# Second graph layer of a GNN and mixture-of-experts kernel: the order of its work on three engines, skewed by one group of tiles

## The reference

```
h = relu(einsum('ts,bsh->bth', adj, x @ Wg0 + bg0))
h = relu(einsum('ts,bsh->bth', adj, h @ Wg1 + bg1))
for p in range(1, MAX_SKIP + 1):
    nw = Tv // p
    wins = h[:, :nw * p, :].reshape(Bv * nw, p, Hd)
    last = _lstm_last(Wih[p - 1], Whh[p - 1], bih[p - 1], bhh[p - 1], wins)
    idx = jnp.arange(nw) * p + (p - 1)
    h = h.at[:, idx, :].set(last.reshape(Bv, nw, Hd))
```

## Time and profile before

| | us |
|---|---|
| median of 3 runs | 1905.67 |
| lowest, highest | 1901.71, 1909.65 |
| the profiled execution | 1909.74 |
| its span, first to last instruction | 1907.9 |
| of it the stage `gnn1` (first gather to end of the last new_state) | 870.31 to 1129.79, 259.5 |
| TensorE, VectorE, ScalarE, POOL busy over the span | 70%, 49%, 34%, 24% |

### The profile page before, as it was taken

One profiled execution on the slowest core, in us unless ns is written; L12 is line 12 of the kernel. 1 busy time (PEld: TensorE's weight loads), 2 busy tenths in 40 slices (PEclk: granted clock), 3 DMA queues, 4 the chain that ended last, 5 costly groups with the idle time before them and its releaser, 6 DMA issues. The chain is left out here.

```text
span 1907.9 us, 25858 instructions
## 1 busy us (share of the span) xinstructions
PE 1332.4 (70%) x5892; PEld 904.9 (47%) x5893; DVE 932.2 (49%) x3988; ACT 655.3 (34%) x1514; POOL 452.5 (24%) x670
## 2 busy tenths in 40 slices
PE   2333410197498999994777779988886998699910
PEld 1223300166466999993434433444333433689910
DVE  6888899776694222223566523333336222701122
ACT  3444400032103455542333335444435433055500
POOL 0000011000004556555655300000000000055556
PEclk9999955596598999996787789999995998599965
DMA  9100000001101222231111000000000100022333
GB/s 264 39 1 1 1 1 1 0 0 54 35 0 38 67 71 68 70 66 50 43 38 37 23 0 0 0 0 1 0 0 11 33 28 17 6 62 70 69 85 100
DMA packets 87126, 69.04 MB, mean 36 GB/s; under 512 B 11158, under 2 KB 77020, under 8 KB 87068
## 3 DMA queue, kind: packets, MB, share of 16 engines
q1 hardware_dynamic: 73884, 41.40, 7.5%
q0 software_dynamic: 13184, 27.03, 6.3%
HBM read 41.38 MB, written 27.00 MB: 36 GB/s over the span
## 5 line engine op out<-in xcount | busy, mean ns | idle before, releaser
L1525 PE MATMUL ps<-BIG,w_ihT 128*128 x364 | 163.1, 591 | 20.7 <-ACT e_go L1547 15.0
L1172 ACT ACTIVATE c_H<-ps,c_b 128x256 f32<-128x256 f32 x284 | 117.4, 471 | 133.2 <-PE ps L1201 132.3
L1122 POOL DMA_INDIRECT c_Z<-z,c_idx x142 | 138.3, 974 | 81.0 <-POOLq L1120 57.4
L1118 POOL COPY g_idx<-sitter 128x1 int32 (+1 forms) x78 | 11.9, 180 | 599.1 <-POOLq L996 583.0
L1312 POOL DMA_INDIRECT d_Y<-y,seat x128 | 128.7, 1005 | 95.7 <-DVE X L1326 49.5
L1214 PE MATMUL ps<-w_dn,c_H 128*128 x1136 | 139.3, 276 | 2.6 <-ACT c_H L1172 2.2
L1201 PE MATMUL ps<-c_ZT,c_w 128*128 128x256 f32 x568 | 136.3, 383 | 1.2 <-ACT c_ZT L1160 1.2
L1214 PEld LDWEIGHTS ps<-w_dn,c_H 128*128 128x128 f32 x1136 | 132.4, 192 | 5.1 <-issue 4.9
L1531 PE MATMUL ps<-e_hs,w_hhT 128*128 128x512 f32 (+1 forms) x256 | 114.2, 590 | 12.9 <-DVE e_hs L1577 12.9
L1525 PEld LDWEIGHTS ps<-BIG,w_ihT 128*128 128x128 f32 x364 | 69.3, 194 | 108.9 <-issue 108.9
L1201 PEld LDWEIGHTS ps<-c_ZT,c_w 128*128 128x128 f32 x568 | 103.6, 192 | 13.4 <-ACT c_ZT L1160 2.1
(11 more groups left out here) (470 smaller groups left out, 2871.4 us busy)
## 6 DMA issues: line engine op xcount, KB each, us to landing
y<-c_ys SPq DMA_DIRECT2D x71, 128.0 KB, 1.8
z<-ZB SPq DMA_DIRECT2D x32, 256.0 KB, 2.3
y<-g_ys SPq DMA_DIRECT2D x39, 128.0 KB, 1.8
out_dram<-X SPq DMA_DIRECT2D x32, 128.0 KB, 1.9
c_Z<-z,c_idx POOLq DMA_INDIRECT x142, 2.6
w_up<-in_L_ffn_W_dram SPq DMA_DIRECT2D x1, 2048.0 KB
w_dn<-in_L_ffn_W_dram SPq DMA_DIRECT2D x8, 256.0 KB
w_dn<-in_L_ffn_Wd_dram SPq DMA_DIRECT2D x8, 256.0 KB
```

The lines of the kernel that those rows point to most:

```text
L1118: pool.tensor_copy(idx[h][u][:, :], k.sitter[:, ds(t * HALVES + h, 1)]).then_inc(copied, 1)
L1122: pool.indirect_dma_start(Z[u][:, h, :], None, z, bass.IndirectOffsetOnAxis(ap=idx[h][u][:, 0:1], axis=0)).then_inc(fetched[u], 16)
L1172: act.activation(H[u][:, c, :], UP[u][c // 2][:, c % 2 * SLOT_TILE:(c % 2 + 1) * SLOT_TILE], ACT.Gelu, bias=(b1[u] if w_up is not None els ...
L1525: last = pe.matmul(o, k.w_ihT[:, w, :], state(i, u, s, p, wide, lanes), start=True, stop=(s == 0))
```

## The change

The same instructions are issued, in another order on three engines; POOL's code is untouched. Iteration g after:
- TensorE: MIX(g), MIX2(g-1), UP(g), GATE(g-1), DN(g);
- ScalarE: ZS(g), HS(g-1), HT(g), gate(g-1), tanh(g-1), normalized(g+1);
- VectorE: the four combines and stats of g with new_state(g-3) behind the first; then add_bias(g-1), new_cell(g-2), scale(g); one iteration more at the end.

Each wait is on the same event as before, with counts shifted to the new place. VectorE:

```
-            for g in range(GROUPS + 2):
+            for g in range(GROUPS + 3):
                 for j in range(GT):
                     if g < GROUPS:
                         combine(g * GT + j)
                         stats(g * GT + j)
-                    if j == 1 and g >= 2:
-                        new_cell(g - 2)
-                    if j == 2:
-                        if g >= 2:
-                            new_state(g - 2)
-                        if 1 <= g <= GROUPS:
-                            add_bias(g - 1)
+                    if j == 0 and g >= 3:
+                        new_state(g - 3)
+                if 1 <= g <= GROUPS:
+                    add_bias(g - 1)
+                if 2 <= g <= GROUPS + 1:
+                    new_cell(g - 2)
                 if g < GROUPS:
                     scale(g)
```

ScalarE, the new loop:

```
+            normalized(0)
+            for g in range(GROUPS + 1):
                 u = g % 2
                 if g < GROUPS:
                     act.wait_ge(mixed, g + 1)
...
                     act.activation(k.ZS[u][:, :], MIX[u][:, :], ACT.Copy).then_inc(mixed_sb, 1)
+                if g >= 1:
+                    act.wait_ge(mix2, g)
...
+                    act.activation(HS[1 - u][:, :], MIX2[:, :], ACT.Relu).then_inc(h2, 1)
                 if g < GROUPS:
                     act.wait_ge(up, g + 1)
...
                     act.activation(HT[u][:, :], UP[:, :], ACT.Relu).then_inc(h_ready, 1)
+                if g >= 1:
+                    gate(g - 1)
+                    act.wait_ge(cell, g)
+                    act.activation(tcs[1 - u][:, :], cs[1 - u][:, :], ACT.Tanh).then_inc(tanh_c, 1)
+                if g < GROUPS - 1:
+                    normalized(g + 1)
```

More of the change, by code:

```diff
@@ L1421, in _ @@
                     act.activation(k.ZS[u][:, :], MIX[u][:, :], ACT.Copy).then_inc(mixed_sb, 1)
-                if 1 <= g <= GROUPS:
-                    act.wait_ge(cell, g)
-                    act.activation(tcs[1 - u][:, :], cs[1 - u][:, :], ACT.Tanh).then_inc(tanh_c, 1)
+                if g >= 1:
+                    act.wait_ge(mix2, g)
+                    if g >= 3:
+                        act.wait_ge(fed, g - 2)
+                    act.activation(HS[1 - u][:, :], MIX2[:, :], ACT.Relu).then_inc(h2, 1)
                 if g < GROUPS:
@@ L1438, in _ @@
                 u = g % 2
+                if g < GROUPS:
+                    pe.wait_ge(z_ready, g + 1)
+                    if g >= 2:
+                        pe.wait_ge(mixed_sb, g - 1)
+                    for j in range(GT):
+                        c = slice(j * P, (j + 1) * P)
+                        last = pe.matmul(MIX[u][:, c], k.ZB[u][:, c], k.BDAT[:, :], start=True, stop=True)
+                    last.then_inc(mixed, 1)
+                if g >= 1:
+                    pe.wait_ge(o_ready, g)
+                    if g >= 2:
+                        pe.wait_ge(h2, g - 1)
+                    for j in range(GT):
+                        c = slice(j * P, (j + 1) * P)
+                        last = pe.matmul(MIX2[:, c], O[1 - u][:, c], k.BDAT[:, :], start=True, stop=True)
+                    last.then_inc(mix2, 1)
+                if g < GROUPS:
+                    pe.wait_ge(mixed_sb, g + 1)
+                    if g >= 1:
+                        pe.wait_ge(h_ready, g)
+                    pe.matmul(UP[:, :], k.w_g1[:, 0, :], k.ZS[u][:, :], start=True, stop=False)
+                    pe.matmul(UP[:, :], k.b_g1a[:, :], k.adjsum[:, :], start=False, stop=True).then_inc(up, 1)
                 if g >= 1:
@@ L1445, in _ @@
                     last.then_inc(fed, 1)
[L1446 to L1473, removed]
+                if g < GROUPS:
+                    pe.wait_ge(h_ready, g + 1)
+                    if g >= 1:
+                        pe.wait_ge(o_ready, g)
+                    for j in range(GT):
+                        c = slice(j * P, (j + 1) * P)
+                        last = pe.matmul(DN[:, c], HT[u][:, c], k.w_g1[:, 1, :], start=True, stop=True)
+                    last.then_inc(dn, 1)
 def windows(n_skip):
```

## The result

The changed kernel takes 1939.82 us, the median of four runs from 1937.37 to 1941.10; the kernel before 1905.70 beside it. The ratio is 1.0178 with a 95% interval of 1.0154 to 1.0201: 34 us slower. The forecast was 1937. The profiled execution after is the fastest of its four (1937.37, span 1935.6), that of before is slower than the other runs of its kernel (1909.74, span 1907.9), so between the two profiles lie only 27.7 us.

The account below looks back on a forecast made before the run. No engine was full; TensorE's serial chain waited 3.6 us a group on round trips. Run 7.82, idle 6.44 and clock 2.75 make a 17.0 us period against 15.03, +31.7 us in all: 1937 us, range 1920 to 1950.

Parts of the forecast that it names:

- The bound and the waits that go: TensorE's stage: no engine full; its waits for ZS, O, HS and HT, 3.6 us a group, go.
- the covers: TensorE steps hiding ZS, HS and HT: MIX2 1.16, UP 2.18, GATE 2.84 us; failing, 0.1 to 0.6 a group shows.
- The chain that comes late: From DN(g) through new_cell, scale and normalized to MIX(g+1): TensorE idles 6.44 us a group.
- The run: TensorE's one unbroken run of matmuls per group: 7.82 us at the higher clock level.
- The clock: Each idle gap drops TensorE to 1.2 GHz for the run's start, adding 2.75 us to each period.
- x: Time into TensorE's run until the higher clock returns: taken as 5.5 us, costing x/2 a period.
- The sum: Whole stage: change of -9.6 + 7.5 x us, +31.7 at x = 5.5, so 1937 us.
- A: Rival: TensorE's clock holds through the gap (x = 0), -9.6 us, 1896; chance 0.04.
- B: Rival: TensorE's higher clock returns only near a run's end or never, +57 to +95 us; chance 0.08, with longer x.
- C: Rival: TensorE's higher clock returns early in the run (x = 3.7), +18 us, 1924; chance 0.16.
- D: Rival: the skew overlaps everything, period falls to POOL's 10.0 us, -75 us, 1830; chance 0.01.

Follow-up runs that it names:

- e2: Changed kernel plus six extra 512-column matmuls behind DN(g), into the UP bank, to hold the clock: ratio 0.9971 to the kernel before, 1938.18 us beside 1943.21.
- e1: Changed kernel with VectorE's scale(g) moved ahead of add_bias(g-1) and new_cell(g-2): ratio 0.9919 to the kernel before, 1927.40 us beside 1943.21.
- e3: Changed kernel with VectorE's order put back to that of before, TensorE's and ScalarE's kept new: ratio 1.0434 to the kernel before, 2027.58 us.
- f2: e4_chain_cut with POOL gathering at most four tiles ahead instead of eight: ratio 0.9682 to the kernel before, 1843.09 us beside 1905.45.
- e4_chain_cut: Changed kernel with VectorE and ScalarE reordered so scale(g+1) and normalized(g+1) need nothing of group g: ratio 0.9878 to the kernel before, 1918.17 us.

## Why the prediction was right

**The bound and the waits that go.** Right. The four round trips of 3.6 us a group vanished, ZS, HS and HT were covered: no wait for them in a steady group. In the changed kernel the lower clock makes the covers longer than costed; e2, all at 2.4 GHz, shows that they hold there too, for ZS by 0.09 us.

**The chain that comes late.** Right, and with the clock that falls in its idle time it is the whole effect. e1 and e3 changed nothing but VectorE's order, and the idle time followed the sum of the instructions in it: 3.97, 6.53 and 10.08 us against 4.0, 6.44 and 10.0 (the first and the last sum were made with 6.53 known). The 0.09 us that was missing in the forecast is that new_cell starts 1.03 after DN's end and not 0.93, since DN ends sooner than taken.

**The run.** Mis-sized a little. It was put at 7.82 us at 2.4 GHz; e2, with the same steps at that level, has it at 7.68. An eight of 128 columns inside an unbroken run takes 1.05 us and the next step starts 0.89 after it starts, where I had used 1.16 and 0.99 from eights that stood behind a wait.

**The clock.** The kind was right, the size was not quite: x is 6.12 us (1103.92 to 1110.04), not 5.5. It was 2.9 in the first run, at the early end (the level is back at 905.24, the run began at 902.31), 4.3 in the second, and grew with every group, with periods of 15.69, 16.21, 16.63, 16.81, 16.93, 17.00, until they stayed at 17.06. What it costs is less than the x/2 of the forecast: 10.53 - 7.68 = 2.85 us and not 3.06, since from one step's start to the next it takes 1.87, 1.71 and 1.84 us at the lower level against 1.00, 0.89 and 1.01 at the higher, not quite double. Neither constant x was true: the forecast's 14 periods were 238.1 us, measured 235.7.

**The sum.** 7.68 + 6.53 + 2.85 = 17.06 against 7.82 + 6.44 + 2.75 = 17.01: the run was too long by 0.14, the idle time and the clock's part too short by 0.09 and 0.10, and these nearly cancelled. The stage came out +29.7 in the profile, forecast +31.7; the medians differ by 34.1. That the forecast of 1937 lies 3 us from 1939.8 is in part luck of that kind: each of its three terms was off by at most 0.14 us a group, but not all to one side.

**The rivals.** A: its mechanism exists, e2 shows its price (0.9971 of before, where 0.995 was its sum), but the clock doesn't hold through 6.5 us of idle time by itself. B: the clock always came back by 6.1 us. C: its x (2.6 to 4.6) was seen in the first two runs only, 2.9 and 4.3. D: needs the chain cut, and then gives 10.44 us a group on a chip without the stall. Its -75 us was -62 in f2, where VectorE waits 12.3 us for gathers and part of the runs is at 1.2 GHz.

The Trainium skill's rule on idle gaps between bursts (TensorE: Matmul & The Clock Gate, "Why this matters for your kernels") held for the changed kernel: the clock was at 0.50 before the end of every gap, while e2, with the gap down to 1.4 us, stayed at 1.00. It doesn't tell the whole: in e1 every second gap of 3.97 us was passed at 1.00, and the kernel before, whose longest wait between steps behind group 0 is 1.5 us, had a mean clock of 0.75.

## What to carry to other kernels

A skew by one group takes the round trips off TensorE, but look for what TensorE's last step of a group now releases: if its reader stands in an in-order queue ahead of the work that feeds the next group's first step, the round trips are not gone, they are one long chain with nothing beside it. Add up the instructions in that queue between the two; here the sum was right to 0.1 us in three kernels. Then add what the clock takes: behind an idle time of 6.53 us in one piece it cost another 2.85 us a group here. Whether the same time in four pieces would cost less wasn't measured; the kernel before, with its four waits, ran at a mean clock of 0.75 as well, the changed one at 0.69.

## What the runs showed of the hardware that I had not expected

The lower clock's share of a run wasn't drawn anew in each group: the periods rose from 15.69 us to 17.06 and stayed there for the last seven to 0.02 us, and those of e1, with an idle time of 3.97, alternated between 13.22 and 14.08.

On two of the chips that were used the same kernel is 38 us (2%) slower than on the others: 11 us of the kernel before's and 19 of the changed kernel's lie in this stage (from MIX(0) on 253.2 against 242.0 and 290.4 against 271.6), where VectorE stands still for up to 21 us while POOL issues gathers without a pause, and some 22 in the last one, which gathers too (from its first gather on 107.5 against 85.2 in the kernel before). MIX(0) starts within 3 us of the same time on all. What comes late there is the rise of semaphores, VectorE's own among them: steps of scale that follow each other in 0.19 us take 1.40 us while POOL gathers. That a kernel which gathers more densely in a stage, as e4_chain_cut does, loses more there is a guess: 0.988 stands for these chips and 0.968 for one without the stall, but with four tiles ahead.
